# A token-by-token tower kernel: routing in groups of four tokens instead of eight

## The chip, the cores and the metric

The kernel runs on one core of a Trainium2 chip. The metric is the device time of one execution in microseconds (us). Three executions of the kernel before took 678.64, 673.30 and 673.35 us; the median is 673.35 us.

## The reference, cut to what matters

128 images are cut into 64 patches each; with a class token that makes 65 tokens per image. Three parts follow one another, all in float32:

```
tokens = patches @ W.T + b, class token in front, times pos_embed      # 128 x 65 x 128
h = tokens + LSTM(layernorm(tokens))                                   # 65 steps, one after another
h = h + MoE(layernorm(h))                                              # 16 experts, the best 2 per row
MoE: probs = softmax(x @ router_w.T + router_b); top 2; 
     out = sum over the two of p_e * (gelu(x @ w1_e.T + b1_e) @ w2_e.T + b2_e)
```

The LSTM is the part that can't be reordered: step n needs the hidden state of step n - 1. The rows of the MoE (65 x 128 = 8320, each to two experts) can be worked on as soon as they are known.

## The kernel before, in words

The program is written by hand, without a scheduler. Each engine has a function `step(n)` and a function `step_b(n)`, and `slots` calls them for slot numbers from -5 upward. An engine runs its instructions in the order in which they are written; between engines there are semaphores alone. So an instruction that waits holds up all that stands behind it on its engine.

**Slots up to 64 are the recurrence.** In slot n the gates of LSTM step n are formed. On TensorE: the recurrent matmuls (L1289, L1294), the transposes of h and of the normalised row (L1304, L1314), the input matmuls of token n + 1 (L1325), the rank matmuls of a routing group if one is due (L1333, L1336), the float32 part of the patch projection of token n + 3 (L1279, 22 records), the transpose of the normalised x of token n + 2 (L1351), the float16 part of the projection (L1279, 24 records), and the router's logits (L1380). ScalarE applies the gates' tanh (L605), the cell's tanh (L626), half of the float16 split, and the conversion of expert weights. VectorE (DVE) forms statistics (L786 to L800), the cell (L804, L807), then what `routing(n)` has for this slot, then the shift (L812) and the normalised x (L821), then the hidden state (L826, L828, L832), then `rest_of_choice(n)`, then the low half of the float16 split (L843), and plan pieces. GpSimd (POOL) computes the low halves of the expert weights (L1209; two pieces in each slot up to 16, one in each from 17 to 48), the power -1/2 of the variances (`rstd`, L1247), the conversion of the slot numbers of a routed group (L1221, L1225), and the sends (L1235).

**Routing.** The tokens are routed in groups. `SIZES` has their sizes, `starting(g)` the slot in which the logits of a group are complete and are read, `slots_taken(g)` over how many slots the twelve steps of the choice of the two experts are spread (L893 to L915), `ready(g)` the slot in which ranks are formed on TensorE and added on DVE (L944, L947), and `routed(g)` the one in which the destinations are formed (L953, L958). Each of the groups 0 to 3 has eight tokens, six slots of choice with two steps in each, ranks in slots 16, 24, 32 and 40, and destinations one slot later. Groups 4 and 5 have eight tokens, four slots with three steps, and rank and destination in one slot (46 and 54). Four smaller groups follow. `routing(n)` emits first the ranks and destinations that are due and then at most three steps of choice; all of that stands ahead of L812, L821 and L826.

**Sends.** Every token is sent twice, each time by one indirect DMA of 128 rows, which GpSimd issues. `send_slots` deals them out: none before the slot after `routed`, at most 2 a slot before slot 48, 3 a slot before slot 64, and 4 from there. In the kernel before they begin in slot 18.

**Slots from 61 on are the tiles.** 80 tiles of 256 rows go through their expert: SyncE loads a tile (L532), TensorE transposes and multiplies it (L1408, L1434, L1452), ScalarE applies gelu, DVE makes the roundings and the result, and GpSimd sends the result rows back (L1257, two per tile). The first 32 tiles are planned from groups 0 to 5 (`EARLY_GROUPS`, plan in slots 54 to 62).

The lines in question are these; the functions stand below.

```
SIZES = [8] * 6 + [6, 4, 4, 3]
EARLY_GROUPS = 6
THIN = 4
```

Of the kernel before, what the change touches and what calls it, by code (L numbers as in the profile page):

```python
# [47 lines left out]
PIECES = E * 2 * FF // PIECE  # L48
TWICE = 16
NE = 7  # L50
UG = 8
SIZES = [8] * 6 + [6, 4, 4, 3]
EARLY_GROUPS = 6
THIN = 4
THREE = 3
EARLY = 32
SINGLE_IN, SINGLE_DOWN = 16, 5
AHEAD = 64
assert EARLY <= -(-(2 * P * sum(SIZES[:EARLY_GROUPS]) - E * (ROWS - 1)) // ROWS)
NX = 4  # L60
# [5 lines left out]
FIRST_SPAN, SECOND_SPAN = 32, 54  # L66
# [31 lines left out]
def tower(nc, x, w, w_rest, cls, pos, w_ih, w_hh, b_ih, b_hh, rw, rb, we, b1, b2, const, out):  # L98
# [3 lines left out]
    with ctx:  # L102
# [214 lines left out]
        R_MASK, R = 12, 16  # L317
        GROUPS = len(SIZES)
        STARTS = np.cumsum([0] + SIZES).tolist()
        def slots(step, tile, steps_first=False):  # L320

            for n in range(-5, AHEAD + TILES_B + 4):
                if n <= AHEAD or steps_first:
                    step(n)
                if n >= AHEAD - 3:
                    tile(n - AHEAD)
                if n > AHEAD and not steps_first:
                    step(n)
# [8 lines left out]
        def place(t):  # L337

            g = max(i for i in range(GROUPS) if STARTS[i] <= t)
            return g, t - STARTS[g]  # L340

        def quick(g):

            return SIZES[g] < UG

        def slot_of(t, usual, *late):

# [11 lines left out]
        def starting(g):  # L359

            return logits_at(STARTS[g + 1] - 1) + 1

        def pieces_at(g):

            return starting(g) + (1 if starting(g) >= AHEAD else 0)

        def slots_taken(g):

            return 2 if quick(g) else 6 if g < THIN else 4

        def ready(g):

            return pieces_at(g) + slots_taken(g)

        def routed(g):

            return ready(g) + (1 if g < THIN else 0)

        def token_at(slots, n):

# [2 lines left out]
        def send_slots():  # L383

            slots, n, room = {}, 0, 0
            for t in range(T):
                for choice in range(2):
                    first = routed(place(t)[0]) + 1
                    if first > n or room == 0:
                        n = max(first, n + 1)  # L390
                        room = 2 if n < PIECES - TWICE else 3 if n < AHEAD else 4
                    slots.setdefault(n, []).append((t, choice))
                    room -= 1
            return slots

        PLAN_A, PLAN_B = ready(EARLY_GROUPS - 1), ready(GROUPS - 1)
        assert PLAN_A + 7 <= AHEAD - 3 and PLAN_B + 8 <= AHEAD + EARLY - 3
# [6 lines left out]
        def through(eng, s, t):  # L404
            eng.wait_ge(s, (t + 1))

        SOFTMAX = ((0, FIRST_SPAN, ready(3) + 4), (FIRST_SPAN, SECOND_SPAN, ready(6) + 2))
        LOADS = {**{at: m for m, at in enumerate(BACK_AT)}, 76: 6, 78: 7, 80: 8}
        STORES = {at + 9: m for m, at in enumerate(BACK_AT)}
        SINGLY, TWO = ((0,), (1,), (2,), (3,), (4, 5)), ((0, 1), (2, 3), (4, 5))  # L410
# [22 lines left out]
        def rows_sent(eng, t):  # L433
            eng.wait_ge(sent_done[t % NP], (t // NP + 1) * 32)
# [7 lines left out]
        def _(sp):  # L442
# [71 lines left out]
            def step_b(n):  # L514
                j = n + 3
                if 0 <= j <= TILES_B - 1:
                    if j == 0:
                        sp.wait_ge(tok_done, (T - 1 - 3))
                        sp.wait_ge(lo_done, (T - 1 - 3))
                        for t in range(STARTS[EARLY_GROUPS] - NP, STARTS[EARLY_GROUPS]):  # L520
                            rows_sent(sp, t)
# [45 lines left out]
        def _(act):  # L567
# [30 lines left out]
            def step(n):  # L598
# [48 lines left out]
                for p in pieces_of(n):  # L647
# [5 lines left out]
                    act.activation(piece, piece, ACT.Copy, scale=E_SCALE).then_inc(ex_hi_done, 1)  # L653
                for k, (t0, t1, at) in enumerate(SOFTMAX):
                    if n == at + 1:
# [58 lines left out]
        def _(dve):  # L714
# [41 lines left out]
            def step(n):  # L756
# [5 lines left out]
                for g in range(GROUPS):  # L762
                    if starting(g) == n:
                        route_logits(g, STARTS[g], SIZES[g])
                t0, t1 = n + 2, n - 1
# [84 lines left out]
                if n == PLAN_B:  # L850
                    dve.wait_ge(r_dve, R * GROUPS)
                    dve.tensor_copy(padi[:, :], count[0:1, :]).then_inc(pad_rows, 1)
                for span, g in enumerate((3, 6)):
                    if n == ready(g) + 1:
                        dve.wait_ge(r_dve, g * R + R_MASK + 2)
                        whole_tiles(plan_a, span)
                for late in (False, True):
                    k = n - (PLAN_B if late else PLAN_A)
                    if 0 <= k <= (6 if late else 8):
                        plan_piece(k, late)  # L860
                for k, (t0, t1, at) in enumerate(SOFTMAX):
                    if n == at:
# [3 lines left out]
            class Group:  # L866
# [50 lines left out]
                def choose(self, a, b):  # L917

                    steps = (*self.find(0, self.L), self.without_first, *self.find(1, self.L2), self.both)
                    assert len(steps) == R_MASK  # L920
                    for step in steps[a:b]:
                        if self.g >= 1 or self.count >= 1:
                            self.seen()
                        step()
# [4 lines left out]
            def route_logits(g, t0, m):  # L929
                dve.wait_ge(logit_ps, (t0 + m))  # L930
                if g == 0:
                    dve.wait_ge(const_in, 16 * N_CONST)
                dve.tensor_tensor(lg[:, t0:t0 + m, :], ps_logits(0, m).rearrange("p (t e) -> p t e", e=E),
                                  rbs[:, 0:m, :], ALU.add).then_inc(r_logits, 1)

            def route_choice(g, t0, m, a, b):
                through(dve, r_logits, g)
                Group(g, t0, m, a).choose(a, b)
# [22 lines left out]
            def rest_of_choice(n):  # L961
                for g in range(GROUPS):
                    k, steps = n - pieces_at(g), R_MASK // slots_taken(g)
                    if 0 <= k < slots_taken(g) and steps > THREE:
                        route_choice(g, STARTS[g], SIZES[g], k * steps + THREE, (k + 1) * steps)

            def routing(n):
                for g in range(GROUPS):
                    if ready(g) == n:
                        route_ranks(g, STARTS[g], SIZES[g])  # L970
                    if routed(g) == n:
                        route_slots(g, STARTS[g], SIZES[g])
                for g in range(GROUPS):
                    k, steps = n - pieces_at(g), R_MASK // slots_taken(g)
                    if 0 <= k < slots_taken(g):
                        route_choice(g, STARTS[g], SIZES[g], k * steps, k * steps + min(steps, THREE))
# [25 lines left out]
            def whole_tiles(s, span):  # L1002

                tiles_of(ceiled[:, span, :], False, ROWS - 1, cst[:, C_EBASE:C_TOK])

            def plan_piece(k, late):
# [17 lines left out]
                if k == 0:  # L1024
                    if late:
                        tiles_of(lengths[:, 2 * E:], late, ROWS - 1, base[2])
                    else:
                        dve.wait_ge(r_dve, R * EARLY_GROUPS)
                        dve.wait_ge(tabs_clear, 1)
# [147 lines left out]
            def add_second(m, a, b):  # L1177
# [7 lines left out]
                if b == size:  # L1185
                    ins.then_inc(add_b, 1)

            slots(step, step_b)

            for m in range(BETWEEN, len(CHUNKS)):  # L1190
# [7 lines left out]
        @block.gpsimd  # L1198
        def _(pool):
            sends = send_slots()  # L1200

            def step(n):
# [11 lines left out]
                for g in range(GROUPS):  # L1214
                    if routed(g) + 1 == n:
                        pool.wait_ge(r_dve, (g + 1) * R)
                        if g >= 4:
                            for k in range(STARTS[g - 4], STARTS[g - 3]):
                                rows_sent(pool, k)
                        m, a = SIZES[g], STARTS[g] % NP  # L1220
                        pool.tensor_copy(slot_own[:, g % 4, :, 0:m], slotf[:, :, 0:m]).then_inc(ids_done, 1)  # L1221
                        for k in range(STARTS[g], STARTS[g + 1]):
                            if k >= NP:
                                rows_sent(pool, k - NP)
                        pool.tensor_copy(pay[:, a:a + m, HID:ROW], tag[:, STARTS[g]:STARTS[g + 1], :]  # L1225
                                         ).then_inc(tagged, 1)
# [274 lines left out]
```

## Time and profile before

| what | value |
|---|---|
| median of three executions | 673.35 us |
| lowest and highest of them | 673.30 and 678.64 us |
| profiled execution, span from its first to its last instruction | 771.4 us |
| mean granted TensorE clock over that span | 0.957 |
| TensorE matmul busy | 647.2 us, 84% |
| VectorE busy | 562.3 us, 73%, 1797 instructions |
| ScalarE busy | 493.0 us, 64% |
| GpSimd busy | 413.1 us, 54%, 446 instructions |
| slots 4 to 8 of the recurrence, from h_hi (L826) to h_hi | 5.72 us each |

The profiled execution lists no time apart from its span, and this span is 98.05 us (14.6%) above the median of the others, so a duration read from it has to be weighed before it is carried over. To read it: the recurrence fills the span from about 20 to 405 us, the tiles from there to 755 us, and the last additions and stores the rest. Up to about 300 us TensorE is never idle. A slot can be found in the trace by its one instruction L826 on DVE: slot n is the (n + 1)th of them.

### The profile page before, as it was taken

How to read it: one execution, taken by the hardware profiler on the slowest of the kernel's cores; microseconds unless marked ns; L12 is line 12 of the kernel's file. 1: busy time of each engine (PE TensorE's matmuls, PEld its weight loads, DVE VectorE, ACT ScalarE, POOL GpSimd, SP SyncE). 2: the span in 40 equal slices, each digit the busy share in tenths (PEclk: the TensorE clock that was granted, in tenths of full speed). 3: DMA queues.
4: the chain of work that ended last, by engine and by line, in shares of the span. 5: the costliest groups of instructions: out<-in, count | busy, mean ns of one | idle time of the engine just before them, and what ended most of it. 6: DMA issues, size and time to landing. Idle time of an engine off the chain costs nothing.

```text
span 771.4 us, 24553 instructions
## 1 busy us (share of the span) xinstructions
PE 647.2 (84%) x7952; PEld 594.7 (77%) x7952; DVE 562.3 (73%) x1797; ACT 493.0 (64%) x1259; POOL 413.1 (54%) x446
## 2 busy tenths in 40 slices
PE   4999999999999999988877665878888787888870
PEld 4999999999999999888875554766666666666660
DVE  3877888888888888778886444756565756677777
ACT  4678876766667666554446343657666767777783
POOL 0243344777767666655656646545555555545552
PEclk9999999999999999999997767999999999999995
DMA  8987877888888887765522222344323234444555
GB/s 318 372 263 271 277 253 251 261 267 256 276 261 267 276 244 236 236 213 182 162 64 60 71 63 73 108 123 119 111 78 98 78 93 118 138 137 131 170 177 195
DMA packets 71895, 141.67 MB, mean 184 GB/s; under 512 B 13078, under 2 KB 55650, under 8 KB 63838
## 3 DMA queue, kind: packets, MB, share of 16 engines
q1 hardware_dynamic: 62128, 121.69, 50.1%
q0 software_dynamic: 9280, 17.21, 6.4%
q8 instruction: 70, 1.15, 0.6%
q10 hardware_dynamic: 366, 1.21, 0.5%
q14 instruction: 51, 0.42, 0.2%
HBM read 116.35 MB, written 25.66 MB: 184 GB/s over the span
## 4 chain that ended last, share of the span: by engine, by line
PE 25%; DVE 24%; another core or an unknown queue 13%; issue 13%; ACT 4%; POOL 3%; DMA 1%; POOLq 0%; ACTq 0%; DVEq 0%; SPq 0%
PE pair L1279 14%; DVE patches L1099 7%; PE pair L1434 3%; DVE patches L1121 2%; PE pair L1325 2%; POOL sent L1235 2%; ACT pair L680 2%; PE pair L1452 2%; PE pair L1289 1%; DVE patches L1114 1%; DVE h L1172 1%; DVE patches L1107 1%; DVE patches L1132 1%; DVE field L843 1%
## 5 line engine op out<-in xcount | busy, mean ns | idle before, releaser
L1257 POOL DMA_INDIRECT back<-patches x160 | 157.0, 981 | 150.6 <-DVE patches L1114 104.6
L680 ACT ACTIVATE pair<-pair,b1s 128x256 f32<-128x256 f32 x320 | 126.3, 448 | 110.4 <-remote 51.5
L1279 PE MATMUL pair<-field,patches 128*128 128x128 f32 (+1 forms) x1408 | 173.9, 280 | 8.9 <-DMA patches<-in_x 8.6
L1279 PEld LDWEIGHTS pair<-field,patches 128*128 128x128 f32 (+1 forms) x1408 | 164.6, 194 | 9.6 <-issue 8.6
L1235 POOL DMA_INDIRECT sent<-pay,slot_own x130 | 149.2, 1148 | 40.3 <-issue 38.2
L1434 PE MATMUL pair<-patches,ex_hi 128*128 128x256 f16 x640 | 119.4, 280 | 47.8 <-DVE patches L1099 23.8
L605 ACT ACTIVATE gate<-pair,lbias 128x128 f32<-128x128 f32 x260 | 74.4, 369 | 98.1 <-PE pair L1294 88.6
L1452 PE MATMUL pair<-ex_hi,patches 128*128 x1280 | 117.4, 225 | 8.3 <-issue 6.1
L1247 POOL TENSOR_TENSOR rstd<-veps,cst 128x2 f32<-128x2 f32 (+1 forms) x68 | 58.0, 853 | 107.2 <-DVE veps L800 106.6
L1107 DVE CAST patches<-pair 128x256 f16<-128x256 f32 x80 | 33.7, 422 | 109.6 <-remote 105.2
L1434 PEld LDWEIGHTS pair<-patches,ex_hi 128*128 x640 | 56.6, 99 | 72.8 <-issue 64.0
L1099 DVE TENSOR_TENSOR patches<-pair,patches 128x1024 f16<-128x1024 f32 x80 | 97.5, 1219 | 5.6 <-ACT patches L689 4.7
L1434 PE MATMUL pair<-patches,ex_lo 128*128 128x256 f16 x320 | 89.2, 279 | 13.6 <-issue 13.5
L1452 PEld LDWEIGHTS pair<-ex_hi,patches 128*128 128x128 f16 x1280 | 90.1, 101 | 13.5 <-issue 9.7
L1279 PE MATMUL pair<-field 128*128 128x128 f16 x1536 | 96.1, 219 | 0.0
L1279 PEld LDWEIGHTS pair<-field 128*128 128x128 f16 x1536 | 91.8, 98 | 0.8
L1452 PE MATMUL pair<-ex_lo,patches 128*128 x640 | 90.8, 225 | 0.0
L587 ACT ACTIVATE field<-patches 128x512 f16<-128x512 f32 x128 | 80.9, 634 | 4.6 <-DMA patches<-in_x 4.6
L689 ACT ACTIVATE patches<-pair 128x1024 f16<-128x1024 f32 x80 | 82.0, 1025 | 2.5
L843 DVE TENSOR_TENSOR field<-patches,field 128x1024 f16<-128x1024 f32 x64 | 78.1, 1221 | 0.1
L1209 POOL TENSOR_TENSOR ex_lo<-field,ex_hi 128x256 f16<-128x256 f32 x64 | 45.5, 720 | 43.3 <-ACT field L653 42.6
L1434 PEld LDWEIGHTS pair<-patches,ex_lo 128*128 x320 | 31.9, 100 | 28.0 <-issue 23.6
(150 smaller groups left out, 1257.7 us busy)
## 6 DMA issues: line engine op xcount, KB each, us to landing
patches<-in_x SPq DMA_DIRECT2D x62, 1152.0 KB
patches<-sent SPq DMA_DIRECT2D x80, 130.0 KB
field<-in_we SPq DMA_DIRECT2D x64, 128.0 KB
field<-back SPq DMA_DIRECT2D x10, 768.0 KB
patches<-in_b SPq DMA_DIRECT2D x80, 64.0 KB
field<-in_pos SPq DMA_DIRECT2D x65, 64.0 KB
out_tower<-h SPq DMA_DIRECT2D x10, 384.0 KB
back<-patches POOLq DMA_INDIRECT x160
```

The costliest lines, as they stand in the source:

```text
L587: return act.activation(xhi[r][:, a:b, :], xraw[q][:, a:b, :], ACT.Copy)
L605: last = act.activation(gate[:, GATE_AT[g], :], ps_gate[n % 2][:, g * B:(g + 1) * B], ACT.Tanh, bias=lbias[:, 2, g:g + 1], scale=(1.0 if g ...
L680: last = act.activation(up[:, cols], up[:, cols], ACT.Gelu, bias=b1s[:, bass.ds(e * FC + 2 * half + i, 1)], scale=1.0 / E_SCALE)
L689: act.activation(hhi[n % 4], pair[n % 2][:, :], ACT.Copy).then_inc(hhi_done, 1)
L843: dve.tensor_tensor(xlo[r][:, :, :], xraw[q][:, 0:KS, :], xhi[r][:, :, :], ALU.subtract).then_inc(lo_done, 1)
L1099: dve.tensor_tensor(hlo[n % 4], pair[n % 2][:, :], hhi[n % 4], ALU.subtract).then_inc(hlo_done, 1)
L1235: pool.indirect_dma_start(sent, bass.IndirectOffsetOnAxis(ap=slot_own[:, g % 4, choice, col:col + 1], axis=0), pay[:, t % NP, :], None, bo ...
L1247: pool.tensor_tensor(rstd[:, both], veps[:, both], cst[:, C_POW:C_POW + 1].to_broadcast([P, both.stop - both.start]), ALU.pow).then_inc(rs ...
L1257: pool.indirect_dma_start(back, bass.IndirectOffsetOnAxis(ap=dsti[j % NO][:, k:k + 1], axis=0), yo[j % NO][:, k, :], None, bounds_check=2 ...
L1279: last = pe.matmul(bank_of, l, w_, start=(c == KS and k == 0), stop=(c == KS - 1 and k == 2))
L1434: last = pe.matmul(ps_up(n, half)[:, i * ROWS:(i + 1) * ROWS], w1, r, start=(k == 0), stop=(k == 2))
L1452: last = pe.matmul(ps_down(j)[:, a * HID:(a + 1) * HID], h, w2, start=(c == 0 and k == 0 and a == 0), stop=(c == FC - 1 and k == 2), skip_ ...
```

## The change

The first 48 tokens are routed in twelve groups of four instead of six of eight; the last four groups stay. Each of the twelve takes four slots for its choice (three steps in each), and rank and destination are formed in the same slot. The number of steps of choice, ranks and destinations of these tokens doubles, each over half as many elements. `ready` falls on slots 10, 14, 18 and so on to 54. Since `starting(g + 1)` is the same slot as `ready(g)` for the first eleven groups, the slots 10, 14, ... 50 hold both the four operations of one group and the first three of the next. The sends begin in slot 11 and are two a slot up to slot 63. The two moments at which whole tiles are counted, and the two at which the softmax starts, are named by the new group numbers: the first count moves from slot 41 to 39 and the first softmax from 44 to 42; the second ones stay in 59 and 60. The plan's slots (54 and 72) stay.

```diff
-SIZES = [8] * 6 + [6, 4, 4, 3]
-EARLY_GROUPS = 6
-THIN = 4
+SIZES = [4] * 12 + [6, 4, 4, 3]
+EARLY_GROUPS = 12
 ...
         def quick(g):
-            return SIZES[g] < UG
+            return g >= EARLY_GROUPS
 ...
         def slots_taken(g):
-            return 2 if quick(g) else 6 if g < THIN else 4
+            return 2 if quick(g) else 4
 ...
         def routed(g):
-            return ready(g) + (1 if g < THIN else 0)
+            return ready(g)
 ...
                     if first > n or room == 0:
                         n = max(first, n + 1)
-                        room = 2 if n < PIECES - TWICE else 3 if n < AHEAD else 4
+                        room = 2 if n < AHEAD else 4
 ...
-        SOFTMAX = ((0, FIRST_SPAN, ready(3) + 4), (FIRST_SPAN, SECOND_SPAN, ready(6) + 2))
+        SOFTMAX = ((0, FIRST_SPAN, ready(7) + 4), (FIRST_SPAN, SECOND_SPAN, ready(12) + 2))
 ...
-                for span, g in enumerate((3, 6)):
+                for span, g in enumerate((7, 12)):
                     if n == ready(g) + 1:
                         dve.wait_ge(r_dve, g * R + R_MASK + 2)
                         whole_tiles(plan_a, span)
```

## Rows read from the trace of the kernel before

**Rows 1.** The page's first line.

```profile
span 771.4 us, 24553 instructions
```

**Rows 2.** The chain of waits, whole span: shares by line.

```profile
by line: PE pair L1279 13.9%; another core or an unknown queue 12.8%; issue 12.6%; DVE patches L1099 7.4%; PE pair L1434 2.8%; DVE patches L1121 2.4%; PE pair L1325 2.2%; POOL sent L1235 1.9%; ACT pair L680 1.8%; PE pair L1452 1.6%; PE pair
```

**Rows 3.** Busy time by window, slots 4 to 8: from:to, length, engines, clock, DMA.

```profile
48.67:77.26 28.59, 28.59 (x377) 28.46 (x376) 22.48 (x82) 22.76 (x71) 10.79 (x15) 1.00 0.79 269
```

**Rows 4.** Timeline of TensorE, slots 26, 28 and 29: start, us, line, operation.

```profile
172.75 0.39 PE L1294 MATMUL pair<-h_lo,whh_hi 128*128 128x128 f16 x4
...
184.62 0.39 PE L1294 MATMUL pair<-h_lo,whh_hi 128*128 128x128 f16 x4
...
188.25 0.27 PE L1351 MATMUL pair<-cst,xn 128*128 128x128 f32 x1
...
190.34 0.39 PE L1294 MATMUL pair<-h_lo,whh_hi 128*128 128x128 f16 x4
```

**Rows 5.** Timeline of TensorE, slot 46 (rank of eight tokens).

```profile
291.13 0.39 PE L1294 MATMUL pair<-h_lo,whh_hi 128*128 128x128 f16 x4
...
292.25 0.22 PE L1333 MATMUL pair<-mask,tri 128*128 128x128 f16 x1
...
292.60 2.70 PE L1279 MATMUL pair<-field,patches 128*128 128x128 f32 x22
295.23 0.33 PE L1351 MATMUL pair<-cst,xn 128*128 128x128 f32 x1
...
297.37 0.39 PE L1294 MATMUL pair<-h_lo,whh_hi 128*128 128x128 f16 x4
```

**Rows 6.** Timeline of VectorE, slot 46: four routing operations between the two.

```profile
293.19 0.29 DVE L807 SCALAR_TENSOR_TENSOR gate<-cab 128x128 f32<-128x128 f32 x1
...
295.08 0.28 DVE L826 SCALAR_TENSOR_TENSOR h_hi<-gate,tc 128x128 f16<-128x128 f32 x1
```

**Rows 7.** Timeline of VectorE, slot 62: the four operations of a group of four.

```profile
401.46 0.29 DVE L807 SCALAR_TENSOR_TENSOR gate<-cab 128x128 f32<-128x128 f32 x1
...
402.46 0.29 DVE L958 TENSOR_REDUCE slotf<-own 128x8 f32<-128x128 f32 x1
402.66 0.15 DVE L812 SCALAR_TENSOR_TENSOR shift<-mv,rstd 128x1 f32<-128x1 f32 x1
```

**Rows 8.** Timeline of VectorE, slot 60: three steps of choice for four tokens.

```profile
387.56 0.29 DVE L807 SCALAR_TENSOR_TENSOR gate<-cab 128x128 f32<-128x128 f32 x1
387.77 0.21 DVE L893 TENSOR_REDUCE top<-lg 128x4 f32<-128x64 f32 x1
...
388.49 0.15 DVE L812 SCALAR_TENSOR_TENSOR shift<-mv,rstd 128x1 f32<-128x1 f32 x1
...
388.81 0.28 DVE L826 SCALAR_TENSOR_TENSOR h_hi<-gate,tc 128x128 f16<-128x128 f32 x1
```

**Rows 9.** Timeline of GpSimd, slots 29 and 30: two sends, one weight piece.

```profile
193.14 1.03 POOL L1235 DMA_INDIRECT sent<-pay,slot_own  x1 [0.19 <-issue]
194.48 1.88 POOL L1235 DMA_INDIRECT sent<-pay,slot_own  x1 [0.30 <-issue]
...
197.78 0.89 POOL L1247 TENSOR_TENSOR rstd<-veps,cst 128x2 f32<-128x2 f32 x1 [0.71 <-DVE veps L800]
```

**Rows 10.** Timeline of GpSimd, slot 12: its two weight pieces.

```profile
96.37 1.40 POOL L1209 TENSOR_TENSOR ex_lo<-field,ex_hi 128x256 f16<-128x256 f32 x2 [2.33 <-ACT field L653]
```

**Rows 11.** Timeline of GpSimd, slot 19, after the first two sends.

```profile
134.51 0.77 POOL L1247 TENSOR_TENSOR rstd<-veps,cst 128x2 f32<-128x2 f32 x1
```

**Rows 12.** Timeline of ScalarE, slot 28: the four gates.

```profile
185.05 1.14 ACT L605 ACTIVATE gate<-pair,lbias 128x128 f32<-128x128 f32 x4 [1.31 <-issue]
```

**Rows 13.** Timeline of all engines, slot 52: gates and a third send.

```profile
327.91 0.97 POOL L1235 DMA_INDIRECT sent<-pay,slot_own  x1 [0.30 <-issue]
...
328.16 0.39 PE L1294 MATMUL pair<-h_lo,whh_hi 128*128 128x128 f16 x4
...
329.69 1.15 ACT L605 ACTIVATE gate<-pair,lbias 128x128 f32<-128x128 f32 x4 [3.03 <-PE pair L1294]
```

## Prediction

> **What bounds the kernel now.** I read the busy time by window first. In slots 4 to 8 TensorE is busy for all of 28.59 us and VectorE for 22.48 [rows 3]: five slots of 5.72 us that TensorE alone sets. The timeline of TensorE then gives the rhythm of one slot: from the last recurrent matmuls (L1294) to the transpose of the normalised x (L1351) 188.25 - 184.62 = 3.63 us of unbroken work, and from there to the next L1294 190.34 - 188.25 = 2.09 us [rows 4]. The sum is 5.72. The reader is to see that L1351 is the one place where VectorE can hold TensorE up: it needs xn (L821), and ahead of L821 stands whatever `routing(n)` has for the slot.
>
> The timeline of VectorE gives the other path to the same place. In slot 46 four operations for eight tokens stand there. From L1294 to the cell (L807) are 293.19 - 291.13 = 2.06 us, from L807 to h_hi 295.08 - 293.19 = 1.89, and L1351 follows 0.15 later: 4.10 us [rows 5, 6]. TensorE alone would have needed 3.63 plus the rank matmuls, 292.60 - 292.25 = 0.35 [rows 5], so 3.98; it waits for about 0.1. That is the model for all that follows: **a slot's wait is 2.06 + (L807 to h_hi) + 0.15, less 3.63 and the rank matmuls.** Behind a waiting TensorE the second stretch takes 297.37 - 295.23 = 2.14 instead of 2.09 [rows 5, 4], 0.05 more.
>
> Last, the chain of waits. 12.8% of the 771.4 us, 98.7 us, are put down to an unknown releaser [rows 2, 1]. The profiled execution is 98.05 us longer than the median of 673.35. Slot 52 shows what that is: L1294 starts at 328.16, ScalarE's gates only at 329.69, 1.53 later [rows 13], where in slot 28 they start 185.05 - 184.62 = 0.43 after it [rows 12, 4]; a third send of GpSimd starts at 327.91, in between. TensorE's signals arrive late while GpSimd issues an indirect DMA. Thirteen of the fifteen slots 48 to 62 have such a lag, worked out in the same way from the two rows of each: 14.2 us together; three earlier slots (27, 35 and 43, of 0.6 to 0.7) have it too. The two numbers near 98 make me take the lag for something that exists in the profiled execution alone. So the sum is made against the span without the lags, and its difference is carried over to the median; I add it to 673.35.
>
> **The change, part by part.**
>
> *Seven operations in one window.* In slots 10, 14, ... 50, eleven of them, the new window holds rank, count, own and slotf of one group of four and the first three steps of choice of the next. In slot 62 the four of a group of four take 402.66 - 401.46 = 1.20 us from L807 to the shift (L812), slotf 0.20 of them [rows 7]. Three steps of choice at four tokens take 388.49 - 387.77 = 0.72 [rows 8]. The first of them needs slotf's completion (0.29 us, and 0.03 for the signal: 0.32 for 0.20) [rows 7]. So L807 to L812 is 1.20 + 0.12 + 0.72 = 2.04, and with 388.81 - 388.49 = 0.32 from the shift to h_hi [rows 8] it is 2.36. The path is 2.06 + 2.36 + 0.15 = 4.57 us. TensorE needs 3.63 and the rank of four tokens: five matmuls for nine, half as wide, about half of 0.35, so 3.81. It waits for 0.76, and loses 0.05 behind: 0.81 a slot, **8.9 us** in eleven slots. Nothing pays it back, since TensorE is the bound in the slots around. Bounds: 4.4 if the wait is half as long because the next slot takes some of it up, 10.5 if the half ranks cost nothing on TensorE.
>
> *The other three slots of each group* have three steps at four tokens: L807 to h_hi 388.81 - 387.56 = 1.25 [rows 8], a path of 3.46 under 3.63. They cost nothing; TensorE's work hides them with 0.17 to spare, and if that cover were gone each would cost up to 0.17.
>
> *Rank matmuls:* six times 0.35 = 2.1 us before, twelve times 0.18 = 2.1 after. Zero.
>
> *Sends that move to slots 11 to 17.* They stand on GpSimd's queue behind the weight pieces and ahead of the next rstd, for which L812 and L821 wait, and behind these all of VectorE. With one weight piece a slot GpSimd has 0.71 us left [rows 9]. Slots up to 16 have two pieces, 1.40 for both, 0.70 each [rows 10]; so it has nothing left, and nothing missing. The first send of all made rstd late already (no wait ahead of it at 134.51 [rows 11]); with a piece more on top I add 0.7 for slot 12, and 0.2 for slot 15, in which L1221 and L1225 come on top. **0.9 us**; bounds 0 and 5.4 (0.9 in each of six slots, if both sends took 1.88 and not 1.03 [rows 9]).
>
> Of the two sends of a slot, one takes 1.03 us and the one beside VectorE's L843 takes 1.88 [rows 9]. The Trainium skill (SBUF — State Buffer, "Who interferes with whom") says that a tensor_tensor with both inputs in SBUF contends with GpSimd's reads, and infers that it leaves the writing of descriptors alone. By that every send would take 1.03, GpSimd would have 0.85 to spare in slots 11 to 16, and this term would be 0; the row says otherwise, and I go by it.
>
> *Sends that leave slots 48 to 63* (three become two): even if the last of three goes beside L843, rstd to rstd is 0.19 + 0.89 + 1.34 + 1.34 + 1.88 = 5.64 (1.34 from send to send [rows 9]), under 5.72, and after slot 48 no weight piece comes on top. VectorE and TensorE cover it. Zero, without the lag. In slots 66 to 68 one send more stands ahead of the first results, while GpSimd waits for VectorE between the slots: zero, bounds -1.3 and 1.3.
>
> *Whole-tile count and softmax* move two slots ahead. The first no longer shares its neighbourhood with L953 and L958 of eight tokens: -0.3, bounds -0.7 and 0.4. The four-operation slots 46 and 54 lose the wait of 0.15 that they have with eight tokens [rows 5]: **-0.3**.
>
> Sum: 8.9 + 0.9 - 0.3 - 0.3 = 9.2; 673.35 + 9.2 = **682.5 us**, 1.4% slower. SyncE's queue isn't passed by anything that moves; its waits for sent rows end earlier.
>
> The Trainium skill (Perfetto Trace Analysis, "Optimizing Scalar/DVE Operations") gives about 60 ns for each DVE instruction on SBUF and advises larger ones where the engine is saturated. The change adds 102 DVE instructions; by that rule the estimate is 6.1 us and 679.5. But VectorE is idle for a fifth of the time here [rows 3]; what costs is that seven stand in one window.
>
> **The rivals.**
>
> *The lag is real* (the other side). Then a third send in a slot costs what the profiled execution shows, in slots 48 to 62. Two sends a slot end earlier than TensorE's signals, and those 14.2 us go. Against that, the slot after a group is routed also sends late and has a lag, three times now, twelve times after. Slots 26 and 27 together take 184.62 - 172.75 = 11.87 [rows 4], 0.43 above two of 5.72; nine more such are about +4.0. 673.35 + 9.2 + 4.0 - 14.2 = **672.4 us**. It decides from the point where a send that is under way at L1294 holds signals back without a profiler. For it: the third send of [rows 13], and that all of the lagging slots but three have three sends. Against it: the 98 us have to go somewhere in the other executions, and nothing else in the trace is longer than its work. If the seven-operation wait is at its lower bound as well, it is 667.9, and with fewer new lags below 666.6. Chance 0.26.
>
> *GpSimd becomes the bound in slots 11 to 16:* the upper bound of that term, 673.35 + 9.2 + 4.5 = **687 us**. For it: nothing left in the queue. Against it: the three operations ahead of L812 cover some of a late rstd. Chance 0.10.
>
> *The seven operations cost half:* 673.35 + 9.2 - 4.5 = **678 us**, within 1%. For it: nothing that I see, slots of such a kind do not exist before. Chance 0.10.
>
> That the change doesn't do what it says is not a case: slots follow from the functions alone.
>
> **How the numbers follow.** My forecast has 0.54, with its own range of 679 to 686. About 1% (6.7 us) is what a measurement here can tell from no change. Slower by over 1%, above 680.1: 0.50 of the forecast and 0.10 of GpSimd, 0.60. Within 1%: 0.04, 0.16 of the real lag and 0.08 of the half cost, 0.28. Faster: 0.10 and 0.02, 0.12. The range reaches from the real lag, 669, to 686; below are about 0.12 and above 0.08.
>
> **What would show it.** In the changed trace: L807 to h_hi at 2.36 in slots 14, 18, ... and L1351 about 0.76 after TensorE ran dry; 5.72 us in the three slots between; L1294 to L605 at 0.43 in slots 48 to 62. The profiled span should even fall, by about 14.2 - 9.2 - 4.0 = 1 us, while the median rises. I am wrong if the eleven slots show no wait of TensorE, or if span and median move together by the lags.

## The result, and the profile after

The changed kernel takes 683.08 us (median of four executions, 681.0 to 683.77), the kernel before 673.33 in the same comparison (671.88 to 678.64). The ratio is 1.0131, interval 1.0098 to 1.0164: about 1.3% slower, where 682.5 us was predicted.

The span shown ahead of the prediction, 771.4 us [rows 1], was that of one unusual execution. The kernel before, profiled a second time without any change (run e0_before), has a span of 671.6 us, and its whole execution takes 673.41, which is in line with the others. This second trace is the one to compare with. The first lines of its page, and then of the page of the changed kernel (busy us, share of the span, instructions):

```profile
span 671.6 us, 24553 instructions
...
PE 620.9 (92%) x7952; PEld 588.9 (88%) x7952; DVE 561.9 (84%) x1797; ACT 489.8 (73%) x1259; POOL 413.0 (61%) x446
```

```profile
span 681.5 us, 24707 instructions
...
PE 623.6 (92%) x7958; PEld 589.1 (86%) x7958; DVE 574.6 (84%) x1899; ACT 490.5 (72%) x1259; POOL 421.9 (62%) x458
```

102 more VectorE instructions, 12.7 us more of VectorE work, and 9.9 us more span. 8.6 of these 9.9 us arise in the recurrence: from L1294 of slot 0 to that of slot 64 are 373.47 us before and 382.09 after (L1294 is L1293 in the changed kernel, and all lines behind it are one lower too). Behind slot 64 are 274.98 and 276.41 us. These 1.4 us can't be put down to the change: over the other traces below that stretch takes 274.4 to 281.0 us.

What happens in a crowded slot is seen in slot 22, the timeline of VectorE (start, us, engine, line, operation; they answer to [rows 6] and [rows 7]):

```profile
154.32 0.29 DVE L806 SCALAR_TENSOR_TENSOR gate<-cab 128x128 f32<-128x128 f32 x1
154.53 0.22 DVE L943 TENSOR_TENSOR rank<-pair,count 128x64 f32<-128x64 f32 x1
154.78 0.17 DVE L946 TENSOR_TENSOR count<-count,pair 128x16 f32<-128x16 f32 x1
154.98 0.29 DVE L952 TENSOR_TENSOR own<-rank,oh 128x128 f32<-128x128 f32 x1
155.31 0.29 DVE L957 TENSOR_REDUCE slotf<-own 128x8 f32<-128x128 f32 x1
155.70 0.22 DVE L892 TENSOR_REDUCE top<-lg 128x4 f32<-128x64 f32 x1
155.95 0.23 DVE L895 TENSOR_TENSOR below<-lg,top 128x64 f32<-128x64 f32 x1
156.21 0.22 DVE L898 SCALAR_TENSOR_TENSOR cand<-below,cst 128x64 f32<-128x64 f32 x1
156.36 0.15 DVE L811 SCALAR_TENSOR_TENSOR shift<-mv,rstd 128x1 f32<-128x1 f32 x1
156.43 0.34 DVE L820 TENSOR_SCALAR xn<-h,mv,rstd 128x128 f32<-128x128 f32 x1
156.68 0.28 DVE L825 SCALAR_TENSOR_TENSOR h_hi<-gate,tc 128x128 f16<-128x128 f32 x1
```

and of TensorE in the same slot (they answer to [rows 4]):

```profile
152.26 0.39 PE L1293 MATMUL pair<-h_lo,whh_hi 128*128 128x128 f16 x4
...
153.38 0.19 PE L1332 MATMUL pair<-mask,tri 128*128 128x64 f16 x1
153.41 0.25 PE L1335 MATMUL pair<-mask,ones 128*128 128x64 f16 x4
153.52 2.70 PE L1278 MATMUL pair<-field,patches 128*128 128x128 f32 x22
156.82 0.33 PE L1350 MATMUL pair<-cst,xn 128*128 128x128 f32 x1 [0.60 <-DVE xn L820]
...
158.97 0.39 PE L1293 MATMUL pair<-h_lo,whh_hi 128*128 128x128 f16 x4
```

From L806 to h_hi are 156.68 - 154.32 = 2.36 us, from L1293 to L1350 156.82 - 152.26 = 4.56, and the slot takes 6.71. TensorE waits for xn, and for nothing else in the slot. L1350 shows 0.60 us of idle time; measured against its place in a slot with the same rank and no wait (3.79 us behind L1293, in e1 below) it comes 0.77 late. All the slots 10, 18, 22, ... 50 take 6.70 or 6.71, and slot 14 takes 6.95; the slots between take 5.72 in nearly every case.

### The profile page after: what moved, and what is told of

It reads as the page before. It is cut to its first block and busy times, and to the rows that moved or that the text cites. A ratio compares the mean times of both kernels' runs of the same rounds, so it can differ in the third digit from the quotient of the medians.

```text
span 681.5 us, 24707 instructions
## 1 busy us (share of the span) xinstructions
PE 623.6 (92%) x7958; PEld 589.1 (86%) x7958; DVE 574.6 (84%) x1899; ACT 490.5 (72%) x1259; POOL 421.9 (62%) x458
## 5 line engine op out<-in xcount | busy, mean ns | idle before, releaser
L1234 POOL DMA_INDIRECT sent<-pay,slot_own x130 | 153.6, 1181 | 43.9 <-issue 43.0
L679 ACT ACTIVATE pair<-pair,b1s 128x256 f32<-128x256 f32 x320 | 123.1, 448 | 29.9 <-PE pair L1433 29.3
L1433 PE MATMUL pair<-patches,ex_hi 128*128 128x256 f16 x640 | 111.0, 275 | 5.7 <-DVE patches L1098 4.0
L1451 PE MATMUL pair<-ex_hi,patches 128*128 x1280 | 111.3, 219 | 2.9 <-DVE patches L1098 1.5
L1451 PEld LDWEIGHTS pair<-ex_hi,patches 128*128 128x128 f16 x1280 | 87.0, 98 | 6.3 <-issue 3.6
L1451 PE MATMUL pair<-ex_lo,patches 128*128 x640 | 88.0, 219 | 0.0
L1433 PE MATMUL pair<-patches,ex_lo 128*128 128x256 f16 x320 | 87.8, 274 | 0.0
L842 DVE TENSOR_TENSOR field<-patches,field 128x1024 f16<-128x1024 f32 x64 | 78.0, 1220 | 0.2
L1208 POOL TENSOR_TENSOR ex_lo<-field,ex_hi 128x256 f16<-128x256 f32 x64 | 48.3, 767 | 33.7 <-ACT field L652 33.2
L1451 PEld LDWEIGHTS pair<-ex_lo,patches 128*128 128x128 f16 x640 | 49.2, 98 | 0.0
```

The source lines that it names most:

```text
L679: last = act.activation(up[:, cols], up[:, cols], ACT.Gelu, bias=b1s[:, bass.ds(e * FC + 2 * half + i, 1)], scale=1.0 / E_SCALE)
L842: dve.tensor_tensor(xlo[r][:, :, :], xraw[q][:, 0:KS, :], xhi[r][:, :, :], ALU.subtract).then_inc(lo_done, 1)
L1234: pool.indirect_dma_start(sent, bass.IndirectOffsetOnAxis(ap=slot_own[:, g % 4, choice, col:col + 1], axis=0), pay[:, t % NP, :], None, bo ...
L1433: last = pe.matmul(ps_up(n, half)[:, i * ROWS:(i + 1) * ROWS], w1, r, start=(k == 0), stop=(k == 2))
L1451: last = pe.matmul(ps_down(j)[:, a * HID:(a + 1) * HID], h, w2, start=(c == 0 and k == 0 and a == 0), stop=(c == FC - 1 and k == 2), skip_ ...
```

## The experiments

**e0, the kernel before once more.** No edit.

> The kernel before, unchanged, profiled once more. If the late signals of TensorE (1.53 us from L1294 to L605 in slot 52) belong to that one profiled execution, its span is now within 1% of 672 us and the gap is 0.43 in slots 48 to 62. If they belong to every profiled execution with three sends a slot, the span is again near 771 us.

Its time was 673.41 us. Slot 52, all engines, answers to [rows 13]: the third send is there again, GpSimd's row at 324.21, and the gates start 324.88 - 324.46 = 0.42 us after L1294, not 1.53.

```profile
324.21 0.97 POOL L1235 DMA_INDIRECT sent<-pay,slot_own  x1 [0.30 <-issue]
...
324.46 0.39 PE L1294 MATMUL pair<-h_lo,whh_hi 128*128 128x128 f16 x4
324.88 1.14 ACT L605 ACTIVATE gate<-pair,lbias 128x128 f32<-128x128 f32 x4 [1.93 <-PE pair L1294]
```

In all slots from 2 to 62 that interval is 0.42 or 0.43, in this trace and in those of the changed kernel and of every other run. So the lag belonged to one execution. Of the 99.8 us between the two spans only 12.1 arose in the recurrence (385.56 against 373.47 us from slot 0 to 64); 87.8 arose behind slot 64, in the tiles. There the granted clock was 0.92 on average instead of 0.97, and TensorE was busy for 266.3 us instead of 243.0: some 23 of the 87.8 us are longer TensorE work, the rest is idle time of TensorE.

**e1, the two groups no longer meet.** A group's choice begins one slot later and takes three slots with four steps (three ahead of the shift, one behind h_lo). The groups of four, the rank slots, the twelve ranks, the sends and the number of VectorE instructions stay as in the change.

```diff
-            return starting(g) + (1 if starting(g) >= AHEAD else 0)
+            return starting(g) + (1 if starting(g) >= AHEAD or not quick(g) else 0)
 ...
-            return 2 if quick(g) else 4
+            return 2 if quick(g) else 3
```

> The changed kernel, but each group of four starts its choice one slot later and takes three slots with four steps each (three ahead of h_hi, one behind); ranks and destinations stay in their slots. Place (seven operations in one window make TensorE wait 0.76 us in eleven slots): the window holds four, the path is 2.06 + 1.52 + 0.15 = 3.73 us under 3.81, the time falls by 8.9 to about 674. Count (102 more VectorE instructions cost time wherever they stand): it stays at 683. Sends (the earlier sends cost it): it stays at 683.

673.31 us (ten executions), ratio to the kernel before 0.9985, interval 0.9959 to 1.0011. The whole loss is gone, with as many VectorE instructions as in the changed kernel (1899). TensorE in slot 22:

```profile
150.05 0.39 PE L1293 MATMUL pair<-h_lo,whh_hi 128*128 128x128 f16 x4
...
151.31 2.70 PE L1278 MATMUL pair<-field,patches 128*128 128x128 f32 x22
153.84 0.27 PE L1350 MATMUL pair<-cst,xn 128*128 128x128 f32 x1
...
155.93 0.39 PE L1293 MATMUL pair<-h_lo,whh_hi 128*128 128x128 f16 x4
```

No wait, 3.79 us to L1350, and a slot of 5.88: 0.16 more than 5.72, which is the price of a rank of four tokens on TensorE. Crowding costs 6.705 - 5.88 = 0.82 us in each of eleven slots, 9.0 together.

**e2, the three steps behind h_hi.** In the eleven crowded slots of the changed kernel the first three steps of choice are issued by `rest_of_choice`, after h_hi and h_lo. Same operations, same slots, another place within the slot.

```diff
+            def crowded(g, k):
+                return k == 0 and 1 <= g < EARLY_GROUPS
 ...
+                    if crowded(g, k):
+                        route_choice(g, STARTS[g], SIZES[g], 0, steps)
 ...
-                    if 0 <= k < slots_taken(g):
+                    if 0 <= k < slots_taken(g) and not crowded(g, k):
```

> The changed kernel with not one instruction more or less: in the eleven slots with seven operations, the three steps of choice stand behind h_hi and h_lo instead of ahead of them. Place: about 674 to 675, as the window is 3.73 us under 3.81. Count: 683. Sends: 683.

677.25 us (nine executions), ratio 1.0048, interval 1.0027 to 1.0070. Most of the loss goes, but less than expected. The crowded slots do take 5.88 (slot 14 takes 6.11). The slot behind each takes 6.06 to 6.09, and slot 43, where the softmax's subtraction comes on top, 7.25. Timeline of VectorE at the border of slots 22 and 23:

```profile
155.96 0.21 DVE L892 TENSOR_REDUCE top<-lg 128x4 f32<-128x64 f32 x1
156.21 0.22 DVE L895 TENSOR_TENSOR below<-lg,top 128x64 f32<-128x64 f32 x1
156.47 0.23 DVE L898 SCALAR_TENSOR_TENSOR cand<-below,cst 128x64 f32<-128x64 f32 x1
156.61 1.22 DVE L842 TENSOR_TENSOR field<-patches,field 128x1024 f16<-128x1024 f32 x1
157.75 0.28 DVE L759 TENSOR_TENSOR xT_lo<-pair,xT_hi 128x128 f16<-128x128 f32 x1
```

and of TensorE:

```profile
157.47 0.39 PE L1299 MATMUL pair<-h_lo,whh_hi 128*128 128x128 f16 x4
157.69 0.28 PE L1309 MATMUL pair<-cst,h 128*128 128x128 f32 x1
158.13 0.30 PE L1319 MATMUL pair<-cst,pay 128*128 128x128 f32 x1 [0.16 <-issue]
```

L1319 writes the other half of the buffer (ps_T) from which xT_lo reads, and the code has it wait for xT_lo. That ends at 157.75 + 0.28 = 158.03; L1319 starts at 158.13, 0.44 behind L1309 instead of 0.11 in a slot without a wait. This is a second place at which VectorE can hold TensorE up. The prediction knew one. One step of choice behind h_lo costs nothing there (e1 has it in every slot of choice); three, 0.65 us from 155.96 to 156.61, cost 0.36.

**e3, the sends as before.** The changed kernel with no send before slot 18, and three a slot from 48 to 63.

```diff
-                    first = routed(place(t)[0]) + 1
+                    first = max(routed(place(t)[0]) + 1, 18)
 ...
-                        room = 2 if n < AHEAD else 4
+                        room = 2 if n < PIECES - TWICE else 3 if n < AHEAD else 4
```

> The changed kernel with the sends of the kernel before: none before slot 18, two a slot to slot 47, three from 48 to 63. Place: only the small term of GpSimd in slots 11 to 15 (0.9) goes, 682. Sends (early sends are what costs): back to 674. If three sends a slot held TensorE back in every execution, it would be 14 us slower than the changed kernel, 697.

682.35 us, ratio 1.0148, interval 1.0103 to 1.0193; the changed kernel had 1.0131 in its own comparison. So the loss is neither that of the early sends (674 expected) nor does a third send a slot cost anything like 14 us (697). The median can't tell e3 from the changed kernel, but the slots can. Slots 12, 13 and 14 take 5.92, 6.01 and 6.95 in the changed kernel and 5.72, 5.72 and 6.71 here: 0.74 us before rounding. GpSimd's queue there in the changed kernel, from the end of slot 12 into slot 13:

```profile
95.75 1.03 POOL L1234 DMA_INDIRECT sent<-pay,slot_own  x1 [0.37 <-issue]
97.09 1.97 POOL L1234 DMA_INDIRECT sent<-pay,slot_own  x1 [0.30 <-issue]
99.08 1.31 POOL L1208 TENSOR_TENSOR ex_lo<-field,ex_hi 128x256 f16<-128x256 f32 x2
100.50 0.82 POOL L1246 TENSOR_TENSOR rstd<-veps,cst 128x2 f32<-128x2 f32 x1
```

There is no idle time ahead of rstd: send, two weight pieces and rstd follow each other. But it is not for rstd that VectorE waits. These are the veps (L799, from which rstd is formed) and the shift (L811) of slot 13 in the changed kernel, and then the veps of the same slot in e3:

```profile
99.77 0.65 DVE L799 TENSOR_SCALAR veps<-mv 128x2 f32<-128x2 f32 x1
...
101.70 0.15 DVE L811 SCALAR_TENSOR_TENSOR shift<-mv,rstd 128x1 f32<-128x1 f32 x1
```

```profile
99.58 0.17 DVE L799 TENSOR_SCALAR veps<-mv 128x2 f32<-128x2 f32 x1
```

rstd is ready at 100.50 + 0.82 = 101.32, before the shift could start in any case. What is late is everything from veps on: the sends have pushed the second weight piece beside veps, which takes 0.65 us instead of 0.17, and from L1293 to the cell (L806) are 2.49 us instead of 2.06. The prediction's formula with 2.49 gives 2.49 + 1.24 + 0.13 - 3.63 + 0.05 = 0.28 us; the slot takes 6.01, 0.29 more than 5.72. In slots 12 and 14 veps takes 0.62 and 0.46, again beside a weight piece.

The send beside VectorE's L842 (96.99 to 98.22) takes 1.97 here and 1.88 in [rows 9]. The Trainium skill (SBUF — State Buffer, "Who interferes with whom") infers that a tensor_tensor leaves the writing of descriptors alone, and by that inference it would take 1.03; the trace disagrees again. What in the send is held up, the writing of descriptors or the reading of its row numbers, no run shows. From slot 48 to 55 both kernels take the same 41.2 us, with two or with three sends a slot; from 48 to 64 the changed kernel takes 95.75 and e3 95.31. The 0.4 us arise in slots 57 to 63, and between e6 and e7 below, which differ by the same sends, the difference there has the other sign.

**e4 and e5, spare operations.** e1 with one (e4) or three (e5) operations that nothing reads, ahead of the shift, in all 36 slots of choice. `spare` is a tile of its own.

```diff
+                        if g < EARLY_GROUPS:
+                            for i in range(1):        # 3 in e5
+                                dve.tensor_tensor(spare[:, i, :], cst[:, 0:2 * E],
+                                                  cst[:, 0:2 * E], ALU.add)
```

> The three-slot version (rank of the next group no longer in the slot in which the group before ends), with one more VectorE operation that nothing reads (128x32, both inputs in SBUF) ahead of the shift in each of the 36 slots with steps of choice. Theory of the path: with 0.20 more the way from L1294 over VectorE is 2.06 + 1.25 + 0.20 + 0.15 = 3.66 us, against 3.74 that TensorE has to do with its normal gap; next to nothing waits. The span grows by 1 us (0 to 2) over the 671.3 of the three-slot version. Theory of counting (every VectorE operation costs its fixed part wherever it stands): 36 x 0.06 = 2.2 us, and with the whole 0.20 of each 7 us.

> The three-slot version with three such operations in each of the 36 slots, so that every slot of choice has six operations there. Theory of the path: 2.06 + 1.25 + 0.60 + 0.15 = 4.06 us (3.99 if the three follow each other closely) against 3.63: a wait of 0.36 to 0.43 and 0.05 behind it in each of 36 slots, some 15.6 us, a span near 687. Theory of counting: 108 x 0.06 = 6.5 us, a span near 678. If the one operation costs nothing and three cost over 10 us, the cost has a threshold: it is what goes beyond TensorE's work.

Spans of 672.0 and 677.3 us (times 673.81 and 679.12). From slot 0 to 64 the three-slot version takes 372.57 us, e4 372.93 and e5 379.60: +0.4 for 36 operations, +7.0 for 108. Three times as many cost far more than three times as much, so there is a threshold. 2.6 of the 7.0 us belong to a collision with a send that e8 takes apart; the 4.4 without it are still over ten times the 0.4 of e4. The sizes came out otherwise than expected. e4 is within its range of 0 to 2 us. For e5 the theory of the path had 15.6 us and the theory of counting 6.5, and by its size alone e5 would speak for counting; it is e4 (2.2 expected by counting, 0.4 measured), e1 and the single slots that refute counting. The path's figure was too high because a spare operation adds 0.10 us and not 0.20 (it depends on nothing, and starts while the one before it ends). Timeline of VectorE in e5, slots 20 and 21:

```profile
143.17 0.39 DVE L979 TENSOR_TENSOR spare<-cst 128x32 f32<-128x32 f32 x3
143.47 0.15 DVE L812 SCALAR_TENSOR_TENSOR shift<-mv,rstd 128x1 f32<-128x1 f32 x1
143.54 0.34 DVE L821 TENSOR_SCALAR xn<-h,mv,rstd 128x128 f32<-128x128 f32 x1
...
148.86 0.28 DVE L906 TENSOR_TENSOR oh<-cst,second 128x64 f32<-128x64 f32 x1
149.06 0.38 DVE L979 TENSOR_TENSOR spare<-cst 128x32 f32<-128x32 f32 x3
149.37 0.15 DVE L812 SCALAR_TENSOR_TENSOR shift<-mv,rstd 128x1 f32<-128x1 f32 x1
149.44 0.52 DVE L821 TENSOR_SCALAR xn<-h,mv,rstd 128x128 f32<-128x128 f32 x1
```

With the durations put right, the prediction's formula gives 2.06 + 1.49 + 0.15 - 3.63 + 0.05 = 0.12 us for slots 19 and 20, 23 and 24 and so on; measured are 0.11. The third slot of each group from slot 13 on takes 6.07, 0.35 more than 5.72 and 0.24 more than its neighbours. There xn takes 0.52, and ends with the first send. Slot 9, the third slot of the first group, comes before any send and takes 5.83 like its neighbours.

**e8, no send there.** e5 without sends in slots 21, 29 and 37.

```diff
+                        if n in (21, 29, 37):
+                            n += 1
                         room = 2 if n < AHEAD else 4
```

> The version with three more VectorE operations a slot, and no send in slots 21, 29 and 37; slots 25, 33, 41, 45, 49 and 53 keep their two. In that version these slots take 6.07 us, the two slots ahead of each only 5.83, though the way from L807 to h_hi is just 0.06 longer in them; their normalised x takes 0.52 us and not 0.34, and ends with the first send. Theory of the collision: without a send the normalised x takes 0.34 again and the slot 0.18 less, 5.72 + (2.06 + 1.55 + 0.15 - 3.63) + 0.05 = 5.90 us in slots 21, 29 and 37, and 6.07 in 25 and 33. Rival, the operations of these slots themselves are longer: 6.07 us in all of them.

TensorE's last recurrent matmuls of slots 21, 22, 23 and of 25 and 26:

```profile
145.74 0.39 PE L1299 MATMUL pair<-h_lo,whh_hi 128*128 128x128 f16 x4
151.57 0.39 PE L1299 MATMUL pair<-h_lo,whh_hi 128*128 128x128 f16 x4
157.59 0.39 PE L1299 MATMUL pair<-h_lo,whh_hi 128*128 128x128 f16 x4
...
169.28 0.39 PE L1299 MATMUL pair<-h_lo,whh_hi 128*128 128x128 f16 x4
175.35 0.39 PE L1299 MATMUL pair<-h_lo,whh_hi 128*128 128x128 f16 x4
```

Slot 21 takes 5.83, slot 25 still 6.07; slots 29 and 37 take 5.83 too. The collision is shown, and it costs 0.24 us and not 0.18, because the operation before the spares, 0.28 above, takes 0.23 again as well; in e5 a send starts 0.02 behind it. Slots 22, 30 and 38 take 0.15 more than in e5: a send now starts together with L955, which takes 0.35 and not 0.29, and xn behind it is caught by the end of the send (0.45 us). The sends left out come later, and the span, 683.9 us, is 6.6 us longer than that of e5. That isn't the collision: the recurrence takes 380.02 us against 379.60, and the stretch behind slot 64 takes 280.95 against 274.42. What makes it longer stays open.

**e6 and e7, a thinner schedule.** e1, and the three whole-tile operations one in each slot from ready + 1 to ready + 3, and the subtraction ahead of the softmax in four quarters of its tokens in four slots. e7 has the sends of e3 as well.

```diff
-                    if n == ready(g) + 1:
+                    if 0 <= n - ready(g) - 1 <= 2:
-                        whole_tiles(plan_a, span)
+                        whole_tiles(span, n - ready(g) - 1)
 ...
-                    if n == at:
-                        below_most(t0, t1)
+                    if 0 <= n - at <= 3:
+                        a, b = (t0 + (t1 - t0) * i // 4 for i in (n - at, n - at + 1))
+                        below_part(a, b, t0, t1, n - at == 3)
```

> The three-slot version with the two other crowded places thinned out too: the three whole-tile operations stand one a slot instead of all in one, and each subtraction ahead of the softmax is cut into four token quarters in four slots. Theory of the path: the slots of that work, 6.30 and 6.62 us in the changed kernel against 5.72 of a slot without a wait, lose most of their 0.58 + 0.90 = 1.48, and slot 58 and 59 some of their 2.9; about 2 us faster than the three-slot version, 671.3. Theory that a wait given back there comes again in the next slot: no change, 673.3.

> The same, and the sends as before the change: none before slot 18, three a slot from 48 to 63. The sends from slot 11 on cost 0.74 us in slots 12 to 14 of the changed kernel; with the seven operations in place, taking them back saved about 1 us at the last timestep and nothing that the median could tell. Expected here: 0 to 1 us less than the run before, 670.5. If the earlier sends help at the end (results waiting for sent rows), it is slower by some tenths instead.

e6 takes 671.66 us (fourteen executions), ratio to the kernel before 0.9969, interval 0.9951 to 0.9986. Its median is the lowest of all versions, though by a third of a percent only, and its interval overlaps with that of e1. e7 takes 672.61, ratio 0.9986, interval 0.9968 to 1.0005: 0 to 1 us less than e6 was expected, and the later sends bring nothing (from slot 0 to 64 they cost 0.67 us more than in e6: 371.46 against 370.78). In slots 40 to 47 e6 saves 0.41 us against e1 and in slots 55 to 63 1.08, 1.5 together where 2 were expected. The quarters of the first softmax are part of it. Timeline of VectorE in e6, three of them, and GpSimd's weight piece beside the first:

```profile
271.87 0.76 DVE L1157 TENSOR_TENSOR lg<-lg,top 128x128 f32<-128x128 f32 x1
...
277.65 0.29 DVE L1157 TENSOR_TENSOR lg<-lg,top 128x128 f32<-128x128 f32 x1
...
283.66 0.76 DVE L1157 TENSOR_TENSOR lg<-lg,top 128x128 f32<-128x128 f32 x1
```

```profile
271.68 0.80 POOL L1227 TENSOR_TENSOR ex_lo<-field,ex_hi 128x256 f16<-128x256 f32 x1
```

All four quarters stand directly behind L843. The second takes 0.29 us, with a send of GpSimd beside it; the other three take 0.76 (the fourth is at 289.50), each beside a weight piece that began 0.2 us before it. The slots behind these three take 6.05, 6.07 and 6.11 (the last has a rank, 5.88 without a wait), the slot behind the short one 5.72. Together that is 0.91 us, where the uncut subtraction cost 0.90 in slot 43 of e1: cutting it up brought nothing there. What e6 saves in slots 40 to 47 comes from the whole-tile operations, 0.42 us.

## Why the prediction was right, point by point

*What bounds the kernel* held. TensorE sets the slots, and L1351 (L1350 after) is where VectorE holds it up. But it is not "the one place": e2 shows xT_lo as a second one.

*Seven operations in one window*, predicted 0.81 us in each of eleven slots and 8.9 in all: measured 0.82 and 9.0 (e1 against the changed kernel). The steps of that term are 2.36 us from L807 to h_hi (2.36 predicted), 4.56 to the transpose (4.57), 3.79 for TensorE alone (3.81), and 0.82 for wait and what is lost behind it (0.81). The rows it was put together from, [rows 7] and [rows 8], are of slots 60 and 62, with other neighbours; that an operation costs there what it costs in slot 22 was the assumption, and it held for the sum. Inside the sum two small errors cancel, which is luck: from slotf to the first step of choice are 0.39 us and not 0.32, and the three steps take 0.66 and not 0.72.

*The other three slots* cost nothing, as predicted: 5.72 us.

*Rank matmuls*, predicted zero: six at 0.37 before, twelve at 0.16 after, so -0.3.

*Sends in slots 11 to 17*, predicted 0.9, measured 0.74 in slots 12 to 14. That the sizes are close is luck, for the way was another: the prediction had L812 and L821 wait for a late rstd, and the traces show rstd in time and veps stretched beside a weight piece, 0.46 to 0.65 us instead of 0.17 (e3). Also not credited: the kernel before pays for its own first sends, in slots 19 and 20 of e0 (6.09 and 5.84 us, 0.49 over two of 5.72), and that goes. In slot 19 send, weight piece and rstd follow each other on GpSimd without a gap, veps takes 0.36 and the cell's second operation (L807) 0.65 instead of 0.29; there the shift does wait for rstd as well, for about 0.1 us. The trace that the prediction was made from has the same two slots (6.09 and 5.84), where the text ahead of it has TensorE never idle. The net is 0.25. The step that failed is this one, by its mechanism and by leaving out the other half of a move: what is moved was counted where it arrives and not where it leaves. It was 0.65 us, too little to be seen in the result.

*Sends that leave slots 48 to 63*: zero, as predicted; e3 differs by 0.4 us over these slots, all of it behind slot 56.

*Whole tiles and softmax*, predicted -0.3: slots 42 and 45 took 6.50 and 6.62 before, 40 and 43 take 6.30 and 6.62 after, -0.2. *Slots 46 and 54*: -0.3 predicted, and -0.3 from 2 x 0.14.

Together 9.0 - 0.3 + 0.25 - 0.2 - 0.3, and 0.1 in the last slots: 8.6 us (8.55 before rounding). From slot 9 to 64 the traces show 322.25 and 330.86 us, a difference of 8.6, where the terms of the prediction were 9.2. The medians differ by 9.75; the interval of the ratio reaches from 6.6 to 11.0 us, so the medians can't tell 8.6 from 9.2.

*The rivals.* The real lag falls with e0. That GpSimd becomes the bound falls with the 0.74 us. That seven operations cost half falls with 0.82. The prediction took the lag for a matter of one execution and carried its sum over to the median, and that was right. It was wrong in expecting the lag in the changed kernel's trace as well, and with it a span near 770: the lag was in that one execution, not in the profiling.

*Counting instructions.* The Trainium skill (Perfetto Trace Analysis, "Optimizing Scalar/DVE Operations") prices each VectorE instruction at about 60 ns of the engine's time, an estimate of 6.1 us for the 102 added here, and says that grouping helps if the engine is saturated. VectorE, busy for 84% of the span, isn't the bound here: e1 has all 102 and loses nothing. The number of operations is no measure of the cost on an engine that isn't the bound; the length of the path in one window is.

## What to carry to other kernels

When an engine off the bound has a fixed place in each period at which the bound waits for it, cost a change by the length of the path up to that place, period by period, and compare it with the work of the bound: up to there operations are free, beyond it each costs its whole length in every period in which they meet. Two lists of due work with the same period must not fall into the same slot: here moving one of them by a slot gave back all of 1.3%. And when work is moved, take the cost off where it leaves, and look at what it now stands beside: here the sends cost time by pushing a GpSimd operation beside a VectorE one.

## What the runs showed of the hardware

A single profiled execution can be 15% longer than all others: 771.4 against 671.6 us of span for the same program, with 1.53 us instead of 0.42 from the start of TensorE's last recurrent matmuls to ScalarE's first gate in slot 52, and a mean granted clock of 0.957 instead of 0.981. What set it off stays open; none of the ten other traces has it.

GpSimd's send and VectorE slow each other in both directions. Which of them loses goes by which starts first. Over all eleven traces, 161 sends start 0.03 to 0.9 us after VectorE's 128x1024 tensor_tensor (1.22 us): 159 of them end 2.05 to 2.07 us after its start, whenever they began, and so take 1.19 to 2.03 us; the first send of all in the two traces of the kernel before takes 2.24. The 404 sends that overlap with it but start before it or together with it take 0.97 to 1.24. A two-input operation that starts 0.02 us before a send takes about 0.06 more (0.28 against 0.23, 0.35 against 0.29). An xn that would have ended 0.90 or 0.97 us after a send's start took 0.52 or 0.45 instead of 0.34, and ended 1.07 to 1.08 after it each time; those that ended 0.82 to 0.87 after it took 0.34. e8 shows the cause by taking the send away; what in a send does it isn't shown.

A VectorE operation beside a GpSimd tensor_tensor of 128x256 can be held up by more than its own length. A 128x128 in-place tensor_tensor takes 0.29 us, and 0.76 there. The tiny veps (tensor_scalar, 128x2) takes 0.15 to 0.17 us in all 708 cases with nothing of GpSimd beside it, and 0.28 to 0.65 in all 20 cases with such a piece beside it. So cutting an operation into pieces can cost as much as it hides.
